# Delta rule: VectorE's last step of the query convolution one turn earlier

## The chip, the cores and the metric

The kernel runs on one core of one Trainium2 chip. Time is the device time of one execution in microseconds; the median of 3 runs is compared. A core has five engines that run their own instruction streams and meet at semaphores: TensorE (PE in the profile, its weight loads PEld), VectorE (DVE), ScalarE (ACT), GpSimd (POOL) and SyncE (SP).

## The reference, cut to what matters

The whole model is four layers, each with an attention-like part and a feed-forward part. The change touches only the attention part of the last layer, a gated delta rule with 8 heads, key width 128, value width 32, here on 8 sequences of 512 tokens (a row each):

```python
q = _causal_dw_conv_silu(x @ Wq, conv_q)     # 4 taps along the tokens, then silu
k = _causal_dw_conv_silu(x @ Wk, conv_k)
v = _causal_dw_conv_silu(x @ Wv, conv_v)
q = _l2norm(q); k = _l2norm(k)
def step(state, inp):
    q_t, k_t, v_t, a_t, b_t = inp
    retained = einsum('bhvk,bhk->bhv', state, k_t)
    state = a4 * (state - b4 * retained[..., None] * k_t) + b4 * v_t[..., None] * k_t
    return state, einsum('bhvk,bhk->bhv', state, q_t)
```

The convolution of the queries is what the moved instruction belongs to: a sum of four shifted copies of the projected row, each times a weight per channel.

## The kernel before, in words

`delta_rule` (from line 1868 on) cuts the layer into 16 units: a unit `u` is one row of 512 tokens and 4 of the 8 heads. A unit has 4 chunks `c` of 128 tokens. A chunk is done in blocks of 9 turns (`NI`, the length of `INVERT`): in one block the triangular matrix of the chunk is built and inverted (`make`, `invert`), in the next block the chunk is solved (`solve`: `state`, then `solve` and `before` in alternation, then `finish`, one step a turn, turns 0 to 8). So block n+1 holds the inversion of chunk n+1 beside the solving of chunk n. Everything else (norms, projections, convolutions, gates, outputs of the units that come next or went before) is cut into pieces, and `pieces_at` puts each piece at a turn and a place. Every engine walks through the same turns with `in_turn` and emits only its own part of each step; in a turn the order is: pieces of place 0, `solve`, `make`, pieces of place 1, `invert`, pieces of place 2. That order, written at build time, is the order of each engine's queue; nothing is reordered later.

The query convolution of one head is spread over a block. With turns counted from the start of the block:

- turn 3: TensorE multiplies the row by the plain query weights into a PSUM bank (L2164).
- turn 4: ScalarE copies the bank, times the weight of the last tap, to the tile `d_conv` (L2291); VectorE adds the tap shifted by 1 (L2441).
- turn 5: VectorE adds the tap shifted by 2 (L2441).
- turn 7, place 2: VectorE adds the tap shifted by 3 (L2441, the form with 509 columns). This is the step that is moved.
- turn 8, place 1: ScalarE takes the silu of `d_conv` into `d_QK` (L2297), GpSimd then squares it (L2246).

There are 64 such convolutions, 4 for each unit, one for each block from the sixth block before chunk 0's until 57 blocks after that. The work around the moved step is, in turn order:

- turn 6: VectorE subtracts into `d_r` (L2400), scales and masks `d_D` and makes `d_A` (L2358, L2361), updates and transposes `d_X` and `d_Y` (L2373, L2375), and scales the values (L2448, place 2). ScalarE then copies `d_A` in four parts (L2260), and GpSimd makes `d_M` from that in two instructions (L2224: 128 columns, then 512).
- turn 7: TensorE solves the last quarter (L2120). VectorE copies it to `d_W` (L2403), multiplies by `gam` to `d_zz` (L2406), and where the chunk is not the last of its unit by `end` to `d_ze` (L2409). TensorE meanwhile has the next inversion product (L2077) and, for three chunks in four, transposes of keys (L2194). In one block of eight VectorE also adds a finished row to `X` here (L2503).
- turn 8: TensorE starts with a tap of the key convolution (L2168), then `finish`: products of `d_zz` (L2126) and, where the chunk is not the last, of `d_ze` (L2130). VectorE adds these to the state `d_S` (L2420; L2414 in a first chunk) and to the output (`d_o` L2421, `d_O` L2423).

The rule that places the convolution is

```python
for x in range(0, 8, 2):
    for j in range(TAPS):
        put(u, NI * (x // 2) - 50 + (0, 0, 1, 3)[j], "conv", TAPS * x + j, place=(1 if j == 0 else 2))
```

where -50 is turn 4 of a block, so the four numbers are offsets from it.

Of the kernel before, what the change touches and what calls it, by code (L numbers as in the profile page):

```python
# [1867 lines left out]
def delta_rule(k):  # L1868

    nc = k.nc  # L1870
    TAPS, NH, NT = 4, 8, 4
    with ExitStack() as s:
# [73 lines left out]
        NI = len(INVERT)  # L1946
        NU, TU = 2 * B, NT * NI

        def pieces_at():

            at = {}

            def put(u, turn, *piece, place=2):
                at.setdefault((TU * u + turn, place), []).append((u,) + piece)

            for turn in range(-6 * NI, NU * TU, NI):
                put(0, turn - 1, "table", 0)
            for u in range(NU):  # L1960
                if u % 2 == 0:
                    for turn, x in ((-55, 1), (-54, 2), (-52, 3)):
                        put(u, turn, "norm", x)
                for turn, piece in ((-36, ("small", 0)), (-35, ("gate", 0)), (-33, ("gate", 1)), (-30, ("gate", 2)), (-24, ("gate", 3)), (-24, ("gate", 4))):
                    put(u, turn, *piece)
                for x in range(5):
                    put(u, x - 9, "norms", x)
                for x in range(32):
                    turn = NI * (x // 8) - 50 + x % 8
                    if x % 8 == 0:  # L1970
                        put(u, turn - 1, "taps", x)
                    elif x % 8 >= 4:
                        put(u, turn, "taps", x, place={8: 0, 0: 0, 1: 1}.get(turn % NI, 2))
                for x in range(0, 8, 2):
                    for j in range(TAPS):
                        put(u, NI * (x // 2) - 50 + (0, 0, 1, 3)[j], "conv", TAPS * x + j, place=(1 if j == 0 else 2))
                for x in range(8):
                    put(u, NI * (x // 2) - 46 + 4 * (x % 2), "taps_done", x, place=(1 if x % 2 == 0 else 2))
                    put(u, NI * (x // 2) - 42 + 2 * (x % 2), "squares", x)
                for x in range(NT):  # L1980
                    put(u, NI * x - 14, "values", x)
                    put(u, NI * x - 13, "values_done", x)
                    put(u, NI * x - 3, "scale", x)
                put(u, 16, "weigh", 0)
                for x in range(NT - 1):
                    put(u, NI * x - 11, "keys", x)
                    put(u, NI * x - 10, "keys_done", x)
                for turn, x in ((9, 0), (11, 1), (12, 2), (13, 3)):
                    put(u, TU + turn, "rms", x)
                if u % 2:  # L1990
                    for turn, x in ((14, 0), (15, 1), (16, 2)):
                        put(u, TU + turn, "out", x)
            return at

        def all_units(name):
# [5 lines left out]
            st = pe, act, dve, pool, dma = k.stage(name)  # L2001
            tmp = OT
            at = pieces_at()
            chunk = lambda u, i: f"u{u}c{i}"

# [796 lines left out]
```

## Time and profile before

| what | value |
|---|---|
| median of 3 runs | 3938.86 us (3933.8 to 3939.21) |
| the profiled execution | 3959.75 us, of which the span is 3958.0 us |
| TensorE busy over the span | 85% |
| VectorE / ScalarE / GpSimd busy | 59% / 43% / 13% |
| delta rule, most of it | from about 2411 us to about 3870 us of the span |

### The profile page before, as it was taken

What the parts mean: (1) busy time and instruction counts of PE and PEld (TensorE: products, weight loads), DVE (VectorE), ACT (ScalarE), POOL (GpSimd) and SP (SyncE); (2) the same over time, 40 slices, a digit from 0 to 9 for tenths busy, and PEclk for the clock granted to TensorE, in tenths of its full rate; (3) what the DMA queues carried; (4) which work ended last, traced back from release to release, by engine and by line L of the source; (5) the groups of instructions that cost most, each with busy time, mean ns of one, the idle gap of its engine ahead of it and who ended that gap; (6) DMA issues with size and microseconds to landing.
All of it is one profiled execution on the core that took longest, in us unless ns stands there. A gap on an engine that the chain in (4) does not pass through costs nothing. (4 is left out here: it accounts for less than half of the span.)

```text
span 3958.0 us, 124996 instructions
## 1 busy us (share of the span) xinstructions
PE 3376.5 (85%) x55256; PEld 2105.7 (53%) x55256; DVE 2329.6 (59%) x6280; ACT 1704.5 (43%) x3930; POOL 528.2 (13%) x532
## 2 busy tenths in 40 slices
PE   3875665689999999999886996999999999999985
PEld 1334553235555545555564443666666666666672
DVE  3766664267767667676882113666666656666545
ACT  1666774364444444344211434443434444434323
POOL 0212331000000000000000001222222222222210
PEclk9897777789989889898665997999999999999967
DMA  2000000221111111110000001000000000000000
GB/s 90 0 0 1 2 2 3 79 67 40 45 42 46 40 32 53 34 45 29 3 3 18 0 5 41 2 3 2 3 2 3 3 2 3 3 2 2 3 2 24
DMA packets 37036, 77.17 MB, mean 19 GB/s; under 512 B 7696, under 2 KB 11152, under 8 KB 35472
## 3 DMA queue, kind: packets, MB, share of 16 engines
q1 hardware_dynamic: 36496, 69.17, 5.5%
q8 instruction: 437, 7.16, 0.7%
q14 instruction: 103, 0.84, 0.1%
HBM read 64.83 MB, written 4.33 MB: 17 GB/s over the span
## 5 line engine op out<-in xcount | busy, mean ns | idle before, releaser
L1401 PE MATMUL ps<-g_hs,g_fc 128*128 128x512 f32 x448 | 271.6, 691 | 53.2 <-DVE g_hs L1715 37.9
L1523 ACT ACTIVATE g_hidden<-ps 128x512 f32<-128x512 f32 x224 | 133.1, 594 | 409.1 <-PE ps L1401 409.0
L1292 PEld LDWEIGHTS ps<-g_Q,g_K 32*32 32x32 f32 x12288 | 204.5, 120 | 182.3 <-issue 95.6
L2168 PE MATMUL ps<-d_hp,d_w_k 128*128 128x512 f32 x512 | 282.1, 637 | 0.0
L1292 PE MATMUL ps<-g_Q,g_K 32*32 32x32 f32 (+1 forms) x12288 | 235.7, 226 | 27.7 <-DVE g_H L1561 10.0
L1415 PE MATMUL ps<-g_hidden,g_proj 128*128 128x512 f32 x448 | 257.3, 662 | 0.0
L2246 POOL TENSOR_TENSOR d_sq<-d_QK 128x512 f32<-128x512 f32 x128 | 133.0, 1039 | 925.1 <-ACT d_QK L2297 763.8
L2266 ACT ACTIVATE d_F<-ps 128x128 f32<-128x128 f32 x256 | 70.8, 276 | 351.3 <-PE ps L2077 348.0
L778 ACT ACTIVATE att_p<-ps,att_mx 128x96 f32<-128x96 f32 x512 | 165.9, 361 | 70.1 <-DVE att_mx L723 64.5
L1260 POOL COPY g_xb<-X 128x512 f32<-128x512 f32 x8 | 7.2, 906 | 1209.8 <-DVE X L1721 1098.5
L2441 DVE SCALAR_TENSOR_TENSOR d_conv<-ps,w_conv_q,d_conv 128x511 f32<-128x511 f32 (+2 forms) x192 | 142.2, 741 | 33.9 <-ACT d_conv L2291 30.0
L2224 POOL TENSOR_TENSOR d_M<-d_A,w_joins 128x128 f32<-128x128 f32 (+1 forms) x128 | 114.3, 912 | 348.0 <-ACT d_A L2260 348.0
L2077 PE MATMUL ps<-d_X,d_M 32*32 32x32 f32 x8192 | 123.8, 196 | 41.4 <-DVE d_X L2373 21.6
L2070 PE MATMUL ps<-d_QK 128*128 128x128 f32 x1024 | 155.5, 297 | 0.0
L2077 PEld LDWEIGHTS ps<-d_X,d_M 32*32 32x32 f32 x8192 | 96.2, 108 | 101.6 <-issue 66.2
L1308 PEld LDWEIGHTS ps<-g_V,g_KT 32*32 32x32 f32 x4096 | 81.8, 121 | 127.7 <-issue 92.8
L2400 DVE TENSOR_TENSOR d_r<-d_r,ps 32x128 f32<-32x128 f32 x192 | 55.0, 286 | 160.6 <-PE ps L2113 89.7
L2260 ACT ACTIVATE d_A<-d_A 32x128 f32<-32x128 f32 x256 | 78.6, 307 | 157.9 <-DVE d_A L2361 153.2
L1549 DVE TENSOR_TENSOR g_S<-g_S,ps 128x128 f32<-128x128 f32 x64 | 18.4, 287 | 215.9 <-PE ps L1308 215.7
L1525 ACT ACTIVATE g_hidden<-g_hidden 128x512 f32<-128x512 f32 x224 | 141.1, 630 | 7.1
L2256 ACT ACTIVATE d_D<-d_D 128x512 f32<-128x512 f32 x64 | 40.3, 629 | 238.1 <-DVE d_D L2348 238.1
L2070 PEld LDWEIGHTS ps<-d_QK 128*128 128x128 f32 x1024 | 130.9, 200 | 21.1 <-DVE d_conv L2441 13.3
(478 smaller groups left out, 7895.1 us busy)
## 6 DMA issues: line engine op xcount, KB each, us to landing
g_hs<-gate_rows SPq DMA_DIRECT2D x56, 256.0 KB, 3.4
g_fc<-in_c_fc_dram SPq DMA_DIRECT2D x56, 256.0 KB, 4.0
g_proj<-in_c_proj_dram SPq DMA_DIRECT2D x56, 256.0 KB, 2.8
X<-in_x_dram SPq DMA_DIRECT2D x1, 2048.0 KB, 10.7
w_c_fc<-in_c_fc_dram SPq DMA_DIRECT2D x1, 2048.0 KB, 8.3
w_c_proj<-in_c_proj_dram SPq DMA_DIRECT2D x1, 2048.0 KB, 12.7
ex_root<-gate_rows SPq DMA_DIRECT2D x1, 2048.0 KB, 15.2
h_rows<-k SPq DMA_DIRECT2D x1, 2048.0 KB, 6.3
```

What stands on the lines that cost most here:

```text
L778: e.activation(p[:, n % 2, i, :], scored[:, g, b], ACT.Exp, bias=mx[:, n % 2, i:i + 1], accum_out=den[:, n % 2, i:i + 1]).then_inc(act.ste ...
L1292: ins = e.matmul(later(scored, n_), keys_, queries(n_, planes, r_, 4 * i + j), start=(turn_ == 0 and part == 0 and n_ != 1), stop=(part == 1),
L1401: e.matmul(P[2], fc[:, n % 2, ts(f, C)], hs[:, n % 2], start=True, stop=True).then_inc(pe.steps, pe.did(now(f"u{i}")))
L1415: e.matmul(P[3], proj[:, n % 2, f, :], r[:, (16 * c["half"] + i) % 5], start=(c["half"] == 0 and i == 0), stop=(c["half"] == 1 and i == 15 ...
L1523: e.activation(r[:, slot], P[2], ACT.Relu).then_inc(act.steps, act.did(now(f"r{i}")))
L1525: e.activation(r[:, slot], r[:, slot], ACT.Square).then_inc(act.steps, act.did(now(f"q{i}")))
L2070: ins = e.matmul(mk[:, ts(h, C)], QK[:, 1, H, t], QK[:, part - 1, H, t], start=True, stop=True)
L2077: ins = e.matmul(inv[rows, h], stationary[rows, h], moving[rows, h], start=True, stop=True, tile_position=(32 * j, 32 * j))
L2168: ins = e.matmul(b, w_k[:, j, ts(H, C)], hp_of(u)[:, j:j + T], start=(j == 0), stop=(j == TAPS - 1))
L2224: e.tensor_tensor(M[:, a, levels], A32[:, a].unsqueeze(1).to_broadcast([C, many, 4, 32]), k.w["joins"][:, levels].unsqueeze(2).to_broadcas ...
L2246: e.tensor_tensor(squares(x), qk, qk, ALU.mult).then_inc(pool.steps, pool.did(f"{tag}sq{x}"))
L2441: e.scalar_tensor_tensor(cv[:, late:], tap_bank(run)[:, 0:T - late], k.w["conv_q"][:, 4 * g + run // 2, 3 - late:4 - late], cv[:, late:], ...
```

## The change

The last of VectorE's three steps of the query convolution gets offset 2 in place of 3: it stands in turn 6, place 2, behind L2448, and no longer in turn 7, place 2, behind L2409. Nothing is added or removed. The other engines keep their order. What waits for the step (the silu in turn 8, and the next use of the PSUM bank in turn 3 of the next block) waits for the same instruction as before.

```diff
                 for x in range(0, 8, 2):
                     for j in range(TAPS):
-                        put(u, NI * (x // 2) - 50 + (0, 0, 1, 3)[j], "conv", TAPS * x + j, place=(1 if j == 0 else 2))
+                        put(u, NI * (x // 2) - 50 + (0, 0, 1, 2)[j], "conv", TAPS * x + j, place=(1 if j == 0 else 2))
```

## Rows read from the trace of the kernel before

**Rows 1.** The page's first line: the span of the profiled execution.
```profile
span 3958.0 us, 124996 instructions
```

**Rows 2.** Windows: stretch, its length, busy time of each engine, PEclk, DMA.
```profile
2440.00:3740.00 1300.00, 1245.37 (x23170) 877.60 (x23169) 799.74 (x2348) 533.98 (x1180) 337.54 (x328) 0.99 0.01 3
```

**Rows 3.** Line L2297 from 2420 to 3740: releaser, then waiters (us, times).
```profile
  DVE d_conv L2441: 73.1, 61
  PEld ps L2077: 0.9, 1
```

**Rows 4.** Timeline, a middle chunk's turns 6 to 8: start, us, engine, line, operation.
```profile
3043.90 0.25 DVE L2448 TENSOR_TENSOR d_values_gates<-d_values_gates,d_kn 128x128 f32<-128x128 f32 x1
3044.18 0.30 DVE L2403 COPY d_W<-ps 32x128 f32<-32x128 f32 x1
3044.52 0.29 DVE L2406 TENSOR_TENSOR d_zz<-d_W,d_gam 128x128 f32<-128x128 f32 x1
3044.56 1.02 PE L2168 MATMUL ps<-d_hp,d_w_k 128*128 128x512 f32 x2
3044.84 0.29 DVE L2409 TENSOR_TENSOR d_ze<-d_zz,d_end 128x128 f32<-128x128 f32 x1
3044.85 0.59 POOL L2224 TENSOR_TENSOR d_M<-d_A,w_joins 128x128 f32<-128x128 f32 x1 [5.56 <-ACT d_A L2260]
...
3045.16 0.75 DVE L2441 SCALAR_TENSOR_TENSOR d_conv<-ps,w_conv_q,d_conv 128x509 f32<-128x509 f32 x1
3045.41 1.26 POOL L2224 TENSOR_TENSOR d_M<-d_A,w_joins 128x512 f32<-128x512 f32 x1
3045.43 0.97 PE L2126 MATMUL ps<-d_zz,d_P 128*128 128x32 f32 x8
3047.33 0.29 DVE L2420 TENSOR_TENSOR d_S<-d_S,ps 128x128 f32<-128x128 f32 x1 [1.42 <-PE ps L2130]
```

**Rows 5.** Timeline, a first chunk whose finish waits for d_ze.
```profile
3108.54 0.29 DVE L2409 TENSOR_TENSOR d_ze<-d_zz,d_end 128x128 f32<-128x128 f32 x1
...
3110.90 0.29 DVE L2414 COPY d_S<-ps 128x128 f32<-128x128 f32 x1 [1.28 <-PE ps L2130]
```

**Rows 6.** Timeline, a last chunk: GpSimd's square and VectorE's L2423 beside it.
```profile
3001.18 1.04 POOL L2246 TENSOR_TENSOR d_sq<-d_QK 128x512 f32<-128x512 f32 x1
3001.44 0.93 DVE L2423 TENSOR_TENSOR d_O<-d_o,d_qn 128x128 f32<-128x128 f32 x1
```

**Rows 7.** Timeline: L2423 of a middle chunk, and L2224 in a last chunk.
```profile
3047.85 0.29 DVE L2423 TENSOR_TENSOR d_O<-d_o,d_qn 128x128 f32<-128x128 f32 x1
3089.05 0.46 POOL L2224 TENSOR_TENSOR d_M<-d_A,w_joins 128x128 f32<-128x128 f32 x1 [5.19 <-ACT d_A L2260]
```

**Rows 8.** Groups by line, VectorE, 2440 to 3740: count, busy us, mean ns, idle.
```profile
L2406 DVE TENSOR_TENSOR d_zz<-d_W,d_gam 128x128 f32<-128x128 f32 x57 | 16.6, 292 | 1.9
L2409 DVE TENSOR_TENSOR d_ze<-d_zz,d_end 128x128 f32<-128x128 f32 x43 | 12.5, 291 | 1.5
```

**Rows 9.** Timeline, the block of eight that adds a row to X.
```profile
3019.02 0.29 DVE L2409 TENSOR_TENSOR d_ze<-d_zz,d_end 128x128 f32<-128x128 f32 x1
3021.71 0.75 DVE L2503 SCALAR_TENSOR_TENSOR X<-ps,mod,X 128x512 f32<-128x512 f32 x1 [2.40 <-PE ps L2207]
3022.38 0.74 DVE L2441 SCALAR_TENSOR_TENSOR d_conv<-ps,w_conv_q,d_conv 128x509 f32<-128x509 f32 x1
...
3022.37 0.86 PE L2126 MATMUL ps<-d_zz,d_P 128*128 128x32 f32 x7
```

**Rows 10.** Windows, finish to finish: three of the same kind of chunk, one late chunk.
```profile
2869.20:2891.85 22.65, 21.58 (x406) 15.72 (x404) 13.90 (x42) 8.75 (x20) 5.17 (x7) 1.00 0.01 2
2691.37:2715.56 24.19, 23.12 (x406) 16.63 (x404) 13.90 (x42) 8.76 (x20) 5.16 (x7) 0.93 0.01 2
3220.12:3245.38 25.26, 24.38 (x405) 17.27 (x404) 13.01 (x42) 8.75 (x20) 5.15 (x7) 0.86 0.01 3
3745.51:3771.66 26.15, 23.58 (x390) 21.54 (x390) 10.95 (x38) 7.05 (x18) 3.07 (x4) 0.61 0.01 3
```

## The prediction, on record before the result

> **What bounds the kernel now.** I read four views in this order: the page's first line, the engines' windows over the delta stage, who waits for the convolution, then the timeline of single blocks.
>
> In the 1300 us from 2440 to 3740 TensorE is busy for 1245.37 us, at a mean clock of 0.99 [rows 2]. So this stage runs at TensorE's pace, and another engine matters only where it makes TensorE stand still. The reader is to see that only 54.6 us of idle are there to be won over 57 or so blocks, and that any new wait of TensorE is added to the time.
>
> The moved step seems to sit on a wait: ScalarE stands idle for 73.1 us in 61 waits, 1.2 us each, until L2441 ends. But nobody passes that on to TensorE: the silus behind it held a weight load up for 0.9 us in all [rows 3]. An earlier convolution is worth nothing by that way.
>
> The timeline shows what the step has around it. In turn 7 VectorE does d_W, d_zz, d_ze without a pause (3044.18 to 3045.13), then the convolution, then it waits 1.42 us for TensorE before d_S [rows 4]. So the step costs nothing where it is: it fills a wait for `finish`. VectorE's d_W, on the other hand, starts 0.03 us behind L2448 (3043.90 + 0.25 = 3044.15): it is held by VectorE's own queue, not by TensorE. Whatever is put between those two delays d_zz and d_ze, and `finish` (L2126) needs them.
>
> **The change part by part.** Removed from turn 7: 0.75 us of VectorE that covers an idle time. After it VectorE waits about 2.2 us for `finish` in place of 1.42. Gain: 0. ScalarE's silu comes earlier, gain 0 by [rows 3] (0.9 us at the most). Added to turn 6: the same 0.75 us between L2448 and d_W. In the one block of eight with the X update the step starts 0.08 us before X ends (3021.71 + 0.75 = 3022.46 against 3022.38) [rows 9], where d_W starts 0.03 us behind. So the instruction behind L2448 starts 0.11 us earlier than d_W does today, and d_W comes 0.75 + 0.03 - 0.11 = 0.67 us later. With no overlap it would be 0.78. I take 0.67.
>
> How much of that TensorE can bear. In a first chunk `finish` waits for d_ze: from the end of d_ze (3108.83) to VectorE's next step 2.07 us pass [rows 5]. In a middle chunk TensorE is still in the tap (3044.56 + 1.02 = 3045.58), and from the end of d_ze (3045.13) to d_S there are 2.20 us [rows 4]. The difference, 0.13 us, is all the cover. In the blocks with the X update d_ze ends at 3019.31 and `finish` starts at 3022.37, 3 us later [rows 9]: cost 0, and DVE's X only moves within that wait.
>
> The blocks that have both a step and a solve number 57: 8 first chunks with no cover, 7 first chunks with the X update, 28 middle chunks, 14 last chunks. The other 7 of the 64 convolutions come before any solve; their order on VectorE doesn't change.
>
> Now d_zz and d_ze move under GpSimd's d_M, and this is the larger part. Row: L2423, a product of two tiles in SBUF, takes 0.29 us alone and 0.93 us when GpSimd's square is running: it ends at 3002.37, 0.15 us behind the square's end (3002.22) [rows 6, 7]. And L2224 takes 0.59 us where d_ze started 0.01 us ahead of it, 0.46 us in a last chunk, which has no d_ze [rows 4, 7]. So the two engines shut each other out, first come first served, for the length of an instruction. d_zz and d_ze have the same form as L2423, and their means of 292 and 291 ns show that none of them meets this today [rows 8].
>
> The Trainium skill (SBUF — State Buffer, Who interferes with whom) says that a VectorE instruction with two SBUF inputs and a GpSimd instruction that reads SBUF exclude each other, and that one with a single SBUF input isn't touched. By it the moved step, which has one operand in PSUM, could run anywhere, while d_zz and d_ze can't; no row here shows d_zz under GpSimd, so the form of L2423 has to stand for it.
>
> Middle chunk, on the clock of [rows 4]: step 3044.07 to 3044.82; d_W 3044.85 to 3045.15; d_zz 3045.18 to 3045.47. L2224's first part is no longer held up and ends at 3044.85 + 0.46 = 3045.31; the second comes in at 3045.27, behind d_zz, which has asked first, and is held some 0.06 us. It ends at 3045.27 + 0.06 + 1.27 = 3046.60. d_ze starts at 3045.51, finds it running, and ends 0.15 us behind it: 3046.75 in place of 3045.13, so 1.62 us late. TensorE loses 1.62 - 0.13 = 1.49 us. First chunk: same distances, no cover, 1.61 us. Last chunk: `finish` needs d_zz alone (0.67 us late, larger cover), and its L2423 already waits for the square [rows 6]; I put 0.1 us.
>
> Sum: 28 x 1.49 + 8 x 1.61 + 14 x 0.1 + 7 x 0 = 41.7 + 12.9 + 1.4 = **56 us**. The bounds of the unknown part, d_zz and d_ze under d_M: not held at all, 28 x (0.67 - 0.13) + 8 x 0.67 + 1.4 = 22 us; both held, one by L2224 and one by the GpSimd instruction behind, 109 us (below). A gain is excluded, since holding can't shorten them. I take the 56, as the order of arrival in [rows 4] gives it, by a margin of 0.09 us.
>
> The clock. A chunk of the same kind lasts 22.65 us at 1.00, 24.19 at 0.93 and 25.26 at 0.86 [rows 10]: a fall to 1.2 GHz costs 1.5 us or more. Falls are rare now (mean 0.99), but in the late chunk, where the taps are gone and TensorE has little to do between waits, the mean is 0.61. The changed blocks get 36 new waits of 1.5 us, each in front of the small products of `finish`, and so come closer to the late one. Ends: no fall more, 0; one in each of 36, 36 x 1.54 = 55 us. I take half of them, **28 us**, since a row on either side is all I have.
>
> The Trainium skill (TensorE: Matmul & The Clock Gate, Why this matters for your kernels) advises against idle gaps clearly longer than the ones forecast here; read so, the clock would hold and the sum stay at 56.
>
> Forecast: +84 us. The profiled execution would go from 3959.75 to 4044, its span from 3958.0 [rows 1] to 4042. It stands 20.9 us over the median of the runs shown, so on the median I put 3938.86 + 84 = **4023 us**.
>
> **The rivals.**
> 1. The clock holds. d_ze waits as above, no more falls: +56, 3995 us. For it: the new waits are short. Against it: [rows 10].
> 2. A plain delay. d_zz and d_ze aren't held, or slip between GpSimd's two parts: +22, 3961 us. For it: no row shows these two tiles held. Against it: L2423.
> 3. A longer chain. L2224's second part comes in before d_zz; then d_zz waits until about 3046.75, and d_ze, starting behind it, for the next GpSimd instruction, the square (1.04 us, free to start since the silu is early), until 3047.73. Middle chunk 2.60 - 0.13 = 2.47 us, first chunk (a 1.26 us instruction there) 2.8, last chunk 1.3: 28 x 2.47 + 8 x 2.8 + 14 x 1.3 = 109 us, with 55 of the clock 164: 4103 us. It is decided by the 0.09 us above.
> 4. Faster: VectorE is late behind `finish`, and the 0.75 us taken out of turn 7 let d_S, d_o and d_Y start earlier. At most 57 x 0.75 = 43 us, 3896 us. It decides where VectorE has no idle time before d_S; it has 1.42 us [rows 4], and 1.28 in a first chunk [rows 5], so it shouldn't.
> 5. No change: TensorE's 54.6 us of other waits [rows 2] take the new one up. They follow from VectorE's work behind `finish` and would move along with it.
>
> **How the numbers follow.** Forecast 47%, rival 1 20%, rival 2 14%, rival 3 11%, rival 4 4%, rival 5 4%. The likeliest case gives 4023 us. Its own range is 56 to 111 us more, 3995 to 4050. The range for 8 in 10 takes in rival 2 with a few us of room and stops short of rival 3: 3958 to 4072. A change under 0.2% (7.9 us) can't be told from none here. Faster 4%, same 4%, slower 92%.
>
> **What would show it.** In the profile after: L2409's mean near 1.2 us in place of 0.291, L2406's still 0.29 (rival 3: 1.4; rival 2: both 0.29). The last-tap L2441 ahead of L2403 in each block, and L2126 waiting for d_ze some 1.5 us in middle chunks. ScalarE's wait of 73.1 us for L2441 almost gone. L2224's smaller form at 0.46 everywhere. The windows' clock in 2440 to 3740 below 0.97 (rival 1: 0.99). Blocks with the X update no longer than now. Wrong would be: d_ze at 0.29, or `finish` no later behind L2120 than now.

## The result and the profile after

| | median us | runs | ratio, 95% interval |
|---|---|---|---|
| before | 3939.03 (3933.8 to 3947.39) | 4 | |
| after | 4144.82 (4133.5 to 4163.67) | 4 | 1.052 (1.0486 to 1.0553) |

The change costs 206 us (4144.82 - 3939.03), not 84. The sign was right; the time lies 73 us above the upper end of the range. (The median of before has a fourth execution in it, and so is 3939.03 and not 3938.86.)

The page's first line and the window of [rows 2] (columns as there) of the kernel after:

```profile
span 4131.7 us, 124996 instructions
...
2440.00:3740.00 1300.00, 1218.33 (x20338) 851.55 (x20338) 721.59 (x2055) 462.83 (x1028) 291.20 (x285) 0.88 0.01 2
```

TensorE is still busy for nearly the whole window (its idle time went from 54.6 to 81.7 us), but it does less in it: the clock fell from 0.99 to 0.88, and VectorE's instructions in 1300 us went from 2348 to 2055. Busy time alone would hide most of this loss.

The groups by line and form (VectorE, then GpSimd; columns as [rows 8]), what ScalarE's silu waits for (as [rows 3]), and TensorE's longest wait in the same window (what waited, releaser, us in total, times, longest):

```profile
L2406 DVE TENSOR_TENSOR d_zz<-d_W,d_gam 128x128 f32<-128x128 f32 x50 | 14.6, 293 | 1.7
L2409 DVE TENSOR_TENSOR d_ze<-d_zz,d_end 128x128 f32<-128x128 f32 x38 | 47.0, 1237 | 1.3
L2224 POOL TENSOR_TENSOR d_M<-d_A,w_joins 128x128 f32<-128x128 f32 x52 | 23.8, 457 | 263.8 <-ACT d_A L2260 263.8
...
  DVE d_conv L2441: 4.0, 2
...
PE ps L2126 <- DVE d_ze L2409: 41.2, 32, 1.6
```

d_zz stayed at 0.29 us, as in [rows 8]; d_ze went from 0.291 to 1.237 us. ScalarE's 73.1 us of waiting [rows 3] are gone, as forecast worth nothing. The third line is GpSimd's small part, at 0.46 us everywhere. A wait of TensorE for d_ze, 1.29 us on average, is new. All of that is the forecast.

The timeline of a middle chunk's turns 6 to 8, the answer to [rows 4]:

```profile
2914.44 0.74 DVE L2441 SCALAR_TENSOR_TENSOR d_conv<-ps,w_conv_q,d_conv 128x509 f32<-128x509 f32 x1
2914.93 1.02 PE L2168 MATMUL ps<-d_hp,d_w_k 128*128 128x512 f32 x2
2915.21 0.30 DVE L2403 COPY d_W<-ps 32x128 f32<-32x128 f32 x1
2915.22 1.74 POOL L2224 TENSOR_TENSOR d_M<-d_A,w_joins 128x128 f32<-128x128 f32 x2 [5.55 <-ACT d_A L2260]
2915.54 0.29 DVE L2406 TENSOR_TENSOR d_zz<-d_W,d_gam 128x128 f32<-128x128 f32 x1
2915.87 1.24 DVE L2409 TENSOR_TENSOR d_ze<-d_zz,d_end 128x128 f32<-128x128 f32 x1
...
2917.16 1.08 PE L2126 MATMUL ps<-d_zz,d_P 128*128 128x32 f32 x8 [1.20 <-DVE d_ze L2409]
...
2919.17 0.29 DVE L2420 TENSOR_TENSOR d_S<-d_S,ps 128x128 f32<-128x128 f32 x1 [2.06 <-PE ps L2130]
```

d_ze starts at 2915.87 while GpSimd's two parts run (2915.22 to 2916.96) and ends at 2917.11, 0.15 us behind them: the tail that L2423 had in [rows 6].

Where the other time went is in the windows from one start of `finish` (L2126) to the next, and one of a stretch at the low clock; columns as in [rows 10]:

```profile
3724.69:3748.38 23.69, 21.60 (x404) 15.64 (x405) 13.97 (x41) 8.76 (x21) 5.13 (x6) 1.00 0.01 3
2917.16:2949.43 32.27, 30.60 (x404) 21.78 (x404) 14.04 (x41) 8.76 (x21) 5.09 (x6) 0.68 0.01 2
2919.20:2939.70 20.50, 20.50 (x200) 14.32 (x194) 6.46 (x24) 2.44 (x8) 1.27 (x1) 0.50 0.01 2
```

The first two are the same kind of chunk. At full clock it takes 23.69 us, 1.04 more than before (22.65, [rows 10]): that is the wait. With a fall of the clock 2 us behind the wait it takes 32.27, for the clock stays at 1.2 GHz for 20.5 us, and that costs 8.58 us, 0.42 us for each us at the low clock. TensorE never pauses in those 20.5 us, and every product of it is longer. Their timeline:

```profile
2919.61 2.08 PE L2168 MATMUL ps<-d_hp,d_w_k 128*128 128x512 f32 x2
2921.48 3.46 PE L2108 MATMUL ps<-d_S,d_QK 128*128 128x32 f32 x16
2924.75 2.06 PE L2062 MATMUL ps<-w_upto,d_g 128*128 128x128 f32 x8
...
2927.30 2.08 PE L2168 MATMUL ps<-d_hp,d_w_k 128*128 128x512 f32 x2
...
2932.83 2.08 PE L2168 MATMUL ps<-d_hp,d_w_k 128*128 128x512 f32 x2
...
2935.40 2.08 PE L2070 MATMUL ps<-d_QK 128*128 128x128 f32 x8
...
2937.99 1.93 PE L2164 MATMUL ps<-d_hp,d_w_q 128*128 128x512 f32 x2
```

The two rows L2070 and L2164 are wide products of turn 3 (wide: 128 or 512 columns on the full array; light: 32 columns, or 32x32 tiles), and there this fall ends. It isn't that no wide product came before them: the key taps (L2168, one row in each turn) and L2062 lie within the stretch, each with light products on either side, and the clock stayed low. The 16 products of L2108 took 1.87 us before. Not every fall lasts until L2070. In a chunk of another kind it began at 2994.3 and ended at 3007.95, behind the third L2168 and just ahead of L2070:

```profile
2994.30:3007.95 13.65, 13.65 (x123) 9.13 (x116) 4.22 (x18) 0.91 (x2) 1.27 (x1) 0.50 0.00 1
...
3001.97 2.08 PE L2168 MATMUL ps<-d_hp,d_w_k 128*128 128x512 f32 x2
...
3005.70 2.08 PE L2168 MATMUL ps<-d_hp,d_w_k 128*128 128x512 f32 x2
...
3008.14 1.05 PE L2070 MATMUL ps<-d_QK 128*128 128x128 f32 x7
```

Here 1.65 us lie between the second and the third L2168, in the stretch above 3.45. For the whole stage, from the first `finish` to the 57th, I counted the falls in the trace's record of the granted clock:

| | stage us | falls | us at 1.2 GHz | mean length |
|---|---|---|---|---|
| before | 1231.7 | 5 | 20.5 | 4.1 |
| after | 1419.2 | 29 | 344.7 | 11.9 |

Of the 29 falls 21 begin 1 to 3 us behind the start of a `finish` that had the new wait, and 20 of these last 10.2 to 20.5 us, 15.4 on average. The other 8 last 3.4 or 6.8 us.

The stage is 187.5 us longer; it starts 13 us earlier (2480.3 against 2493.5), which the change doesn't explain: the other traces start it anywhere from 2473.1 to 2491.4. The profiled executions lie 174 us apart and not 206 (4131.7 - 3958.0): the one of after was the fastest of its four, that of before stood 21 us over its median. The shares below are of the profiled executions; the 18 us by which the medians go beyond the stage's 187.5 are placed by no trace.

### The profile page after: what moved, and what is told of

Read it like the earlier page. It is cut to its first block and busy times, and to the rows that moved or that the text cites. A ratio compares the mean times of both kernels' runs of the same rounds, so it can differ in the third digit from the quotient of the medians.

```text
span 4131.7 us, 124996 instructions
## 1 busy us (share of the span) xinstructions
PE 3508.3 (85%) x55256; PEld 2187.8 (53%) x55256; DVE 2355.8 (57%) x6280; ACT 1704.5 (41%) x3930; POOL 526.8 (13%) x532
## 5 line engine op out<-in xcount | busy, mean ns | idle before, releaser
L2168 PE MATMUL ps<-d_hp,d_w_k 128*128 128x512 f32 x512 | 332.9, 741 | 0.0
L2441 DVE SCALAR_TENSOR_TENSOR d_conv<-ps,w_conv_q,d_conv 128x511 f32<-128x511 f32 (+2 forms) x192 | 141.9, 739 | 34.0 <-ACT d_conv L2291 31.8
L2070 PE MATMUL ps<-d_QK 128*128 128x128 f32 x1024 | 157.7, 300 | 0.0
L2224 POOL TENSOR_TENSOR d_M<-d_A,w_joins 128x128 f32<-128x128 f32 (+1 forms) x128 | 111.4, 892 | 346.3 <-ACT d_A L2260 346.3
L2108 PEld LDWEIGHTS ps<-d_S,d_QK 128*128 128x128 f32 x768 | 134.7, 264 | 34.1 <-issue 17.0
L2070 PEld LDWEIGHTS ps<-d_QK 128*128 128x128 f32 x1024 | 132.7, 202 | 24.4 <-DVE d_conv L2441 15.1
```

Source lines behind the costliest of these rows:

```text
L2070: ins = e.matmul(mk[:, ts(h, C)], QK[:, 1, H, t], QK[:, part - 1, H, t], start=True, stop=True)
L2108: ins = e.matmul(b[:, half * 128 + 32 * h:half * 128 + 32 * h + 32], QK[:, what, 4 * (u % 3) + h, ts(c, C)], S[:, 4 * g + h], start=True, ...
L2168: ins = e.matmul(b, w_k[:, j, ts(H, C)], hp_of(u)[:, j:j + T], start=(j == 0), stop=(j == TAPS - 1))
L2441: e.scalar_tensor_tensor(cv[:, late:], tap_bank(run)[:, 0:T - late], k.w["conv_q"][:, 4 * g + run // 2, 3 - late:4 - late], cv[:, late:], ...
```

## The experiments

The theory: d_ze makes TensorE wait 1.0 to 1.6 us in front of `finish`; behind such a wait come mostly light products, the clock falls and stays low for the 10 to 20 us until turns 1 to 4. Its rivals: VectorE's later order itself costs the time; or the convolution's early end does (GpSimd's square, ScalarE's silu); or it takes many waits together. All ratios are to the kernel before, with runs of it on the same chip (medians 3948.8, 3948.4 and 3946.7 in the three batches).

**e1_square_later.** The kernel after, with GpSimd's second d_M held until d_ze is done.

```diff
+ was = 4 * u + c - 2
+ if l == 1 and was >= 0:
+     e.wait_ge(dve.steps, dve.at(f"z{chunk(was // NT, was % NT)}"))
```

> The changed kernel, with GpSimd's second and longer d_M instruction made to wait until VectorE has ended d_zz and d_ze. Theory (the wait of TensorE before finish is made by d_ze standing behind GpSimd, and the clock falls because of that wait): L2409 back at 0.29 us, the wait 0.5 to 0.7 us in place of 1.5, its own cost 28 x 0.53 + 8 x 0.67 = 20 us; the clock falls much more seldom than the 28 times of the changed kernel; together +20 to +60 us against before, 3960 to 4000 us. Rival A (the 0.67 us shift of d_W is enough to bring the falls, GpSimd has no part): mean clock still near 0.88, 4090 us or more. Rival B (the falls don't cost time of their own): only the 25 to 36 us of shorter waits are won back, 4105 to 4120 us.

1.0221 (1.018 to 1.0261): 4035.21 us. TensorE's wait for d_ze in 2440 to 3740, and d_ze itself:

```profile
PE ps L2126 <- DVE d_ze L2412: 12.1, 35, 0.7
...
L2412 DVE TENSOR_TENSOR d_ze<-d_zz,d_end 128x128 f32<-128x128 f32 x41 | 12.0, 292 | 1.4
```

That GpSimd lengthens d_ze is shown: held back, it leaves d_ze at 0.292 us. The time is above what I expected, for the plain delay of 0.35 us a block (12.1 / 35) still came with 12 falls and 184 us at 1.2 GHz.

**e2_fill.** The kernel after, with two wide products in place of the wait ahead of `finish`; their result is overwritten.

```diff
+ if c < NT - 1 and 4 * u + c <= 56 and (c or g or not u):
+     e.wait_ge(dve.steps, dve.at(f"w3{n}"))
+     for _ in range(2):
+         e.matmul(b[:, 0:352], k.w["ones3"][:], w_q[:, 0:352], start=True, stop=True)
  e.wait_ge(dve.steps, dve.at(f"z{n}"))
```

> The changed kernel with two extra matmuls of 352 columns each (some 1.2 us) on TensorE in the stretch in which it waits for d_ze, in first and middle chunks; their product is thrown away, and the output stays as it is. All else as in the changed kernel, d_ze still 1.24 us. Theory (the time beyond 45 to 56 us comes from the granted clock, which falls because TensorE stands idle ahead of the light products of finish): the falls go, mean clock from 2440 to 3740 back to 0.97 or more, +45 to +65 us against before, 3984 to 4004 us, although TensorE does more work. Rival (the lost time is in the waits and their chain, the clock only shows them): 4145 us or more, since the waits are unchanged and work is added.

1.0152 (1.0117 to 1.0187): 4005.49 us, some 140 less than after, with more work. The window of [rows 2], and the timeline of the filler (L2127; L2130 is `finish` here):

```profile
2440.00:3740.00 1300.00, 1247.45 (x22536) 867.92 (x22534) 801.09 (x2265) 510.89 (x1133) 320.68 (x313) 0.99 0.01 2
...
2871.65 1.34 PE L2127 MATMUL ps<-d_w_q,w_ones 128*128 128x352 f32 x4
2873.02 1.08 PE L2130 MATMUL ps<-d_zz,d_P 128*128 128x32 f32 x8
```

`finish` starts as late as in the kernel after, d_ze is as long, VectorE's order is the same; only TensorE's idle time is filled. The clock is back at 0.99, with 5 falls and 20.5 us, just as before. This parts the loss in two: the stage is 51.5 us longer than before (1283.2), which is the waits, and the other 136 us of the 187.5 are the clock (136 / 324.2 = 0.42 us for each us more at 1.2 GHz, the price of the two chunks above once more).

**e3_late_finish.** The order of before; `finish` in the 36 blocks waits for a fill of an unused tile that VectorE does in idle time.

```diff
  e.wait_ge(dve.steps, dve.at(f"z{n}"))
+ if c < NT - 1 and 4 * u + c <= 56 and (c or g or not u):
+     e.wait_ge(dve.steps, dve.at(f"late{n}"))
  ...
+     e.memset(idle[:, 0:900], 0.0).then_inc(dve.steps, dve.did(f"late{n}"))
  e.wait_ge(pe.steps, pe.at(f"o{n}"))
```

> The kernel before, with the convolution step where it was, but finish in first and middle chunks waits for one more VectorE instruction (a memset of an unused tile, 900 columns) placed behind that step, so that TensorE stands idle about as long as in the changed kernel (1.5 to 1.6 us) with nothing of VectorE ahead of d_W and no meeting with GpSimd. Theory (only the length and the place of TensorE's wait matter): the same clock as the changed kernel (0.88) and about its time, 4110 to 4160 us. Rival (GpSimd's and VectorE's meeting, or the earlier silu and table load, are a cost of their own): +45 to +60 us, about 3990 us, with a clock of 0.97 or more.

1.0563 (1.0503 to 1.0622): 4168.11 us, a little above the expected range. The window, and the waits of a part of it (2700 to 3400):

```profile
2440.00:3740.00 1300.00, 1214.49 (x19798) 850.84 (x19797) 702.18 (x2041) 456.88 (x1014) 289.92 (x281) 0.87 0.01 2
...
PE ps L2129 <- DVE d_idle L2415: 25.2, 17, 1.8
```

With the convolution where it was, d_ze at 0.29 us and 36 waits of 1.5 us (25.2 / 17), the loss is there in full: the wait alone makes it, without the moved step and without GpSimd's lengthening.

**e4_last_only** and **e5_first_only.** One head's convolution of four moved. With `x == 4` it is the one beside the last chunks of the units, with `x == 6` the one beside the first chunks.

```diff
- put(u, NI * (x // 2) - 50 + (0, 0, 1, 3)[j], ...)
+ put(u, NI * (x // 2) - 50 + (0, 0, 1, 2 if x == 4 else 3)[j], ...)   # e5: x == 6
```

> The change for one convolution of four only, the one whose block solves the last chunk of a unit (14 blocks). Theory: d_zz comes 0.67 us later there but finish has 0.46 us of cover and L2423 waits for the square anyway; the changed kernel shows 0.2 us a chunk, so +3 us, 3942 us, clock as before. Rival (each moved step costs its share of the 206 us, 57 blocks alike): 14/57 x 206 = +51 us, 3990 us.

> The change for one convolution of four only, the one whose block solves a first chunk (15 blocks, of which 8 bear the wait and 7 have the X update). Theory (a 1.6 us wait ahead of finish, then a fall that lasts until the dense products of turns 3 and 4): waits 8 x 1.57 = 13 us; behind the waits of the odd units, where the changed kernel fell for 13.7 us each time, falls of 10 to 14 us for most of 7, some 6 us each, 42 us; together +40 to +60 us against before, 3980 to 4010 us. Rival (a fall needs the waits of many blocks together): +13 us and no more falls than the 4 or 5 of before.

e4: 1.0004 (0.9986 to 1.0022), 3946.55 us over 10 runs, no difference; 4 falls. That rules out the rival by which the early convolution costs by itself. In its trace the two windows of eight that end with a last chunk's `finish` take 21.64 us in place of 21.54, which is the 0.1 us that the prediction had. e5: 1.0177 (1.0146 to 1.0208), 4015.11 us, 67 more, above what was expected. TensorE's waits in e5:

```profile
PE ps L2126 <- DVE d_ze L2409: 12.8, 8, 1.6
```

The 8 waits are 1.6 us each, as the prediction had them (1.61), and 12.8 us in all; the rest comes with 12 falls and 126 us at 1.2 GHz.

**e7_one_in_eight.** As e3, but only where `(4 * u + c) % 8 == 1`.

```diff
- if c < NT - 1 and 4 * u + c <= 56 and (c or g or not u):
+ if (4 * u + c) % 8 == 1 and 4 * u + c <= 56:
```

> The kernel before, in which finish waits some 1.5 us for a memset behind the convolution step in one block of eight only (that of the second chunk of an even unit), 8 blocks in all. Theory (one wait is enough for a fall, and the light stretch behind finish keeps the clock at 1.2 GHz until turn 4): 8 x 1.4 = 11 us of waits and up to 7 falls of 17 to 20 us, 8.6 us of time each, up to 60 us: +40 to +70 us, 3985 to 4015 us. Rival (the falls build up over blocks, the clock answers to the mean load): +11 us, clock 0.98 or 0.99.

1.0114 (1.0083 to 1.0145): 3991.16 us. Seven blocks have the wait (9.9 us in 7), and four of them were followed within 3 us by a fall of 10.2 to 23.9 us; the longest as a window:

```profile
2870.60:2894.50 23.90, 23.90 (x221) 16.88 (x220) 6.49 (x24) 4.36 (x12) 1.26 (x1) 0.50 0.01 1
```

The waits of this kernel are 180 us apart, so one is enough; but the other three had none behind them. The same wait in the same program doesn't always bring a fall.

**e8_wait_in_turn4.** The order of before, with a wait of the same blocks in another place: TensorE's value products in turn 4, which are wide, wait for VectorE's first step of the convolution.

```diff
+ if 0 <= n_ <= 56 and n_ % 4 < 3 and (n_ % 8 or not n_):
+     e.wait_ge(dve.steps, dve.at(f"u{v}conv{8 * i + 1}"))
```

> The kernel before, the convolution step where it was, no wait ahead of finish; in the 36 blocks of first and middle chunks TensorE waits in turn 4, ahead of the value products (128 columns, full array, L2153), for VectorE's first step of the query convolution, some 1.4 us, about as long as in the changed kernel. Theory (the place of the wait counts: behind it come 8 x 128 full columns, which bring the clock back or keep it): waits 36 x 1.4 = 50 us, few falls or falls of 3.4 us: +50 to +80 us, clock 0.96 or more, 3990 to 4025 us. Rival (every idle time of this length brings the same falls wherever it lies): +150 to +220 us, clock 0.88.

1.0238 (1.0202 to 1.0274): 4035.08 us, 87 more where at most 80 were expected. The window, and the waits of 2700 to 3400:

```profile
2440.00:3740.00 1300.00, 1186.97 (x22034) 839.39 (x22035) 745.42 (x2221) 499.33 (x1108) 316.61 (x307) 0.98 0.01 2
...
PE ps L2158 <- DVE d_conv L2446: 35.5, 18, 2.8
```

These waits are longer than those of e3 (1.97 against 1.48 us on average) and cost 87 us instead of 219. The idle time itself is seen here in the busy column (1186.97). The clock kept at 0.98: 16 falls, 14 of them of 3.4 us and two of 6.8.

**e10_fill_behind.** The kernel after with the wide products of e2 not in the wait but some 4 us behind it (2907.73 - 2903.45), at the head of the state step in turn 0.

```diff
+ was = 4 * u + c - 1
+ if 0 <= was <= 56 and was % 4 < 3 and (was % 8 or not was):
+     for _ in range(2):
+         e.matmul(b[:, 0:352], k.w["ones3"][:], w_q[:, 0:352], start=True, stop=True)
```

> The changed kernel with two extra matmuls of 352 columns behind finish instead of ahead of it: in turn 0, before the products of the state step (L2108), in the 36 blocks that follow a wait. Their product is thrown away. The waits for d_ze stay. Theory (the clock stays at 1.2 GHz for 10 to 20 us because only light products follow the fall; dense work behind it brings the clock back): falls still come, but most last 3.4 to 7 us, 100 to 150 us at 1.2 GHz in the stage in place of 345; 85 to 110 us won, 36 x 1.2 = 43 us or somewhat more of added work: 4080 to 4105 us, 40 to 65 us under the changed kernel. Rival (how long a fall lasts doesn't hang on what follows it): as many us at 1.2 GHz, 4190 us or more.

1.0393 (1.0363 to 1.0423): 4096.19 us, 49 less than after with the waits still there. The window, and the timeline of one block (L2130 is `finish`, L2107 the filler):

```profile
2440.00:3740.00 1300.00, 1211.48 (x20990) 838.17 (x20988) 742.66 (x2109) 477.14 (x1060) 298.39 (x291) 0.95 0.01 2
...
2903.45 1.08 PE L2130 MATMUL ps<-d_zz,d_P 128*128 128x32 f32 x8 [1.20 <-DVE d_ze L2413]
...
2907.73 1.94 PE L2107 MATMUL ps<-d_w_q,w_ones 128*128 128x352 f32 x4
2909.51 1.87 PE L2112 MATMUL ps<-d_S,d_QK 128*128 128x32 f32 x16
```

L2112, which took 3.46 us in the kernel after, is back at 1.87: the clock is up again behind the filler, which stands right behind a wide tap. There are 32 falls, but none longer than 6.8 us (mean 4.3), 136.5 us in all. With the same waits there are about as many falls (32 and 29); what TensorE has behind them set how long they last.

**e11_late_short.** As e3 with a fill of one column, so that the wait is 0.57 us on average (20.0 us in 35) and 0.9 at the most.

```diff
-     e.memset(idle[:, 0:900], 0.0)...
+     e.memset(idle[:, 0:1], 0.0)...
```

> The kernel before, the convolution step in its place, and finish in first and middle chunks waits for that step and a memset of one column: a wait of 0.7 to 0.9 us where e3_late_finish makes one of 1.6. Theory (a longer wait makes more falls, out of proportion to its length): waits 8 x 0.85 + 28 x 0.7 = 26 us, low time between the 188 us of e1_square_later (wait 0.5 us) and the 345 of the changed kernel: +100 to +150 us, 4045 to 4095 us. Rival (falls in proportion to the length of the wait): half of what e3_late_finish lost, +110 us, with half its 396 us; then the two can't be told apart, and the clock's share is all that is learned. Rival B (below about 1 us no falls come): +26 us.

1.0271 (1.0231 to 1.0311): 4041.99 us; 19 falls, 164 us at 1.2 GHz, mean clock 0.94. Some two fifths of the wait make a little under half the loss. Both are less than was expected (188 us or more at the low clock, +100 us or more), and e1, with shorter waits (0.35 us), has more low time (184 us) than this. So the length of the wait alone doesn't set the low time, and how the loss grows with it stays open; only that a short wait is harmless is ruled out.

**e9_x_first** and **e12_fill_turn1** looked for a kernel faster than before. e9 puts VectorE's first inversion step ahead of the four d_D; e12 fills a wait in turn 1 with one product.

```diff
+ if part == 0 and not now and (u or c):          # e9, in make
+     return
...
+ m = NT * u + c + 1                              # e9, behind d_Y and its transpose
+ if m < NU * NT:
+     make(m // NT, m % NT, 0, now=True)
```

```diff
+ if l == 1 and u + c:                            # e12
+     e.matmul(P[0][:, 0:128], k.w["ones3"][:], w_q[:, 0:128], start=True, stop=True)
```

> The kernel before, with one other order on VectorE alone: in turn 0 the first inversion step (d_Y, d_X, L2368 and L2370) goes ahead of the four d_D instructions (L2348) instead of behind them. TensorE waits for d_X in turn 1 in the light stretch today (0.3 to 0.45 us in 28 or more blocks); d_D has cover, since GpSimd's mask ends 3 us before it is used. Theory (each wait of TensorE in the light stretch costs its length, and the clock falls behind it): 10 to 20 us faster, and fewer than the 5 falls of before, another 0 to 9 us: 3915 to 3935 us. Rival (the wait is replaced by the one for d_D or for the copy to d_W behind it, as one queue serves both): no change within 0.2%.

> The kernel before with one extra matmul of 128 columns on TensorE in turn 1 of each block, ahead of the first inversion product, where TensorE waits 0.3 to 0.4 us for d_X. It fits into that wait. Theory (the 5 falls of before, 20 us at 1.2 GHz, come in the light stretch of turns 0 to 2 and go with a little more work there): up to 9 us faster, 3930 to 3948 us against 3948. Rival (the added instruction delays the product where the wait is shorter than it): 0 to 8 us slower.

e9: 0.9997 (0.9975 to 1.0018), 3947.63 us; some kinds of chunk got 0.26 us shorter, one 0.5 us longer (23.05 to 23.58), and the expected 10 to 20 us didn't come. e12: 0.9998 (0.998 to 1.0017), 3945.99 us; one fall of 3.4 us was left in the stage, which was 9.6 us shorter in the profiled execution, but the whole time doesn't show it. The 5 falls of before are worth too little to be won back.

**All runs together.** At 0.42 us for each us at the low clock, from the pair of chunks above, the rest of each stage should be the waits and the fillers alone:

| kernel | stage against before | low time against before | x 0.42 | rest | TensorE's new waits, us |
|---|---|---|---|---|---|
| after | +187.5 | +324.2 | 136 | 51 | 44.8 in 35 |
| e1 | +87.0 | +163.8 | 69 | 18 | 11.8 in 35 |
| e2 | +51.5 | 0 | 0 | 51.5 | filled |
| e3 | +215.0 | +375.5 | 158 | 57 | 52.3 in 35 |
| e5 | +53.5 | +105.8 | 44 | 9 | 11.2 in 7 |
| e7 | +34.1 | +54.6 | 23 | 11 | 9.9 in 7 |
| e8 | +76.1 | +41.0 | 17 | 59 | 68.0 in 35 |
| e10 | +145.9 | +116.0 | 49 | 97 | 44.8, and 35 fillers x 1.34 = 47 |
| e11 | +81.4 | +143.4 | 60 | 21 | 20.0 in 35 |

The rest follows the waits within 9 us everywhere, so one price does for all these kernels, as a mean: other pairs of equal chunks in the kernel after give 0.44 (27.79 and 21.75 us, 13.7 low) and 0.50 (23.92 and 22.22 us, 3.4 low). (The first of the 36 blocks begins the stage, so that its wait lies outside.)

## Why the prediction was wrong

1. **What bounds the stage, right.** Each new wait of TensorE went into the time, and ScalarE's lost wait brought nothing.
2. **The mechanism of the wait, right.** d_zz at 0.29 and d_ze at 1.24 us, waiting for GpSimd by order of arrival with the 0.15 us tail. The Trainium skill (SBUF — State Buffer, Who interferes with whom) says this of a VectorE instruction with two SBUF inputs, and that one with a single SBUF input, as the convolution step, goes free. The traces agree: in [rows 4] L2441 took 0.75 us beside GpSimd's second part, where d_ze took 1.24. The shutting out isn't for the whole recorded length, though: d_zz started 0.14 us before GpSimd's first part ended (2915.54 against 2915.22 + 0.46), and neither of them was longer for it.
3. **56 us of waits, right.** Measured 51.5 in e2, 51 by the table. A first chunk's wait was 1.60 us (1.61 forecast); a middle chunk lengthened by 1.04 us and the one behind an X update by 1.37 (1.49 forecast): `finish` comes 2.23 us behind the start of the tap (2917.16 - 2914.93) in place of 0.87 [rows 4], 1.36 later, and a part of that came back in the small waits of TensorE (for VectorE's L2370 12.8 us in 35 before, 8.7 in 22 after, over the stage). Last chunks: 0.10 us each in e4's trace, as forecast, too little to show in its time.
4. **28 us for the clock, wrong: 136.** This is the step that failed. It was 18 falls at 1.54 us. The number was near: 24 more, and 21 of the 29 stand behind one of the 36 waits. As half of 36 was a guess between two ends, that is luck. The size of a fall was mis-sized: the price came from one 3.4-us fall of [rows 10], and the 20 long ones last 15.4 us on average (over all, 324.2 / 24 = 13.5 us more at the low clock for each more fall, x 0.42 = 5.7 us of time). Even one fall for each of the 36, at the old price, made only 55, so the upper bound was none. Four of the five falls of before came in the middle of a block, shortly ahead of the wide products of turn 3, and ended there:

```profile
2691.37:2701.80 10.43, 10.01 (x166) 8.15 (x165) 5.40 (x20) 3.42 (x5) 3.55 (x4) 1.00 0.01 2
2701.80:2705.20 3.40, 3.40 (x17) 2.05 (x16) 0.79 (x5) 0.00 (x0) 0.00 (x0) 0.50 0.02 5
2705.20:2715.56 10.36, 9.71 (x226) 6.43 (x225) 7.72 (x18) 5.34 (x15) 1.61 (x3) 1.00 0.01 2
```

   These are windows of the kernel before, of the chunk that [rows 10] has at 0.93: the fall begins 10.4 us behind `finish` and lasts 3.4. The long new ones begin 1 to 3 us behind `finish`, with the work of turns 0 to 2 still ahead, light products with one wide tap (L2168) in each turn, and this work takes longer still at half the clock. The row that told of this stood in [rows 10] as its last: a chunk of light products at 0.61. I took it for the ground that falls might come, and not for what they cost there.
5. **Blocks with the X update no longer than now: half right.** At full clock they are the same (22.26 before, 22.22 after), but 6 of the 7 had a fall of 3.4 us, where one had it before, and took 23.92. They have no new wait of their own; why they fall wasn't tried.
6. **Rivals.** The clock holds (+56) is what e2 makes by filling the waits, not what the kernel does. The Trainium skill (TensorE: Matmul & The Clock Gate, Why this matters for your kernels) warns of idle gaps longer than these; here gaps of 0.35 to 1.6 us ahead of light products came with 12 to 34 falls (e1, e3), so the measurement decides against reading it as safe. A plain delay and the longer chain are refuted by d_ze and d_zz. A gain from VectorE's emptied turn 7 isn't seen: it waited 2.06 us for `finish` in place of 1.42. That the other waits take the new one up (rival 5) is refuted by the 51.5 us of e2. The sum of rival 3 comes to 110 and not 109 (69.2 + 22.4 + 18.2); nothing hangs on it.

## What to carry to other kernels

When a change puts a short wait in front of small products on a busy TensorE, price it twice: the wait, and the time that the clock would stay low behind it, times the cost of a us at the low clock (0.42 us here). How long it stays low goes by the work behind the wait: 10 to 20 us here, 3.4 to 6.8 with two more wide products there (e10). A price taken from the falls that a profile already has holds only for falls in the same place. And where a VectorE instruction with two SBUF operands feeds TensorE, look at what GpSimd starts beside it before moving anything ahead of it.

## What was not expected of the hardware

- A busy TensorE can stay at the low level: TensorE was 100% busy for 20.5 us at 1.2 GHz (20.50 of 20.50 us above), three single wide taps among light products included, and the clock came back only at L2070 and L2164; behind one wait of 1.4 us it was low for 23.9 us (e7).
- The same idle time is cheap ahead of wide products: 36 waits of some 1.9 us cost 87 us in e8, 36 of 1.5 us cost 219 in e3.
- Adding work made the kernel faster: two 352-column products a block took some 140 us out (e2), because they stood where TensorE had waited.
- What decides whether one and the same wait is followed by a fall stays open: 4 of 7 in e7, and in the kernel after the pattern repeats (falls at 2714.4, 2919.2 and 3124.0, each of 20.5 us and 204.8 apart, where the `finish` ahead of each lies 2 us earlier), which speaks against mere chance. Whether it's the place in time of the wait was tested by no run.
